# Moving the third row of max scores ahead of the value products in the second attention's loop

## The reference

```python
scores = jnp.einsum('bhqd,bhkd->bhqk', q, k) / math.sqrt(HD)
causal = jnp.tril(jnp.ones((Sx, Sx), dtype=bool))
scores = jnp.where(causal, scores, -jnp.inf)
aw = jax.nn.softmax(scores, axis=-1)
aw = aw.reshape(Bx, NQ, 2, Sx, Sx)
aw = aw[:, :, 0] - lam * aw[:, :, 1]
attn = jnp.einsum('bhqk,bhkd->bhqd', aw, v) * (1.0 - LAMBDA_INIT)
```

## Time and profile before

| | us |
|---|---|
| median of 3 runs | 597.56 (595.37 to 598.63) |
| the profiled execution | 598.44 |
| its span, first to last instruction | 596.7 |

### The profile page before, as it was taken

The page is one execution under the profiler, slowest core; times in us unless marked ns, Lnnn a source line. Parts: engine busy times, 40 slices in busy tenths (PEclk is TensorE's granted clock), DMA queues, the critical chain, the costliest instruction groups (busy, mean ns, idle before and its releaser), DMA issues.

```text
span 596.7 us, 12939 instructions
## 1 busy us (share of the span) xinstructions
PE 515.9 (86%) x3948; PEld 364.4 (61%) x3948; DVE 429.4 (72%) x1668; ACT 328.9 (55%) x544; POOL 311.7 (52%) x472
## 2 busy tenths in 40 slices
PE   4978559967589999999999999998797899999960
PEld 2657459955256444544444544445486799999960
DVE  4785746636859899999999999994859445455436
ACT  4744326622573577777777777775620444454523
POOL 3541055417634586665685667566500577677630
PEclk9998759988699899999999999999969899999995
DMA  8400112322672546557635543431930111111215
GB/s 326 203 2 19 53 37 72 70 75 56 125 133 56 105 99 132 128 108 173 161 80 123 136 120 88 86 80 38 331 102 19 37 49 50 49 48 50 45 33 206
DMA packets 90496, 58.20 MB, mean 98 GB/s; under 512 B 72673, under 2 KB 76770, under 8 KB 88614
## 3 DMA queue, kind: packets, MB, share of 16 engines
q1 hardware_dynamic: 81550, 41.18, 27.4%
q0 software_dynamic: 3744, 7.68, 5.1%
q10 hardware_dynamic: 5136, 8.52, 4.1%
HBM read 37.72 MB, written 19.63 MB: 96 GB/s over the span
## 4 chain that ended last, share of the span: by engine, by line
PE 73%; DVE 15%; DMA 4%; ACT 3%; issue 3%; POOL 2%; ACTq 0%; SPq 0%; POOLq 0%; DVEq 0%
PE banks L1140 15%; PE banks L1984 13%; PE banks L1972 11%; PE banks L1958 11%; PE banks L1153 9%; DVE banks L1675 3%; PE banks L1924 1%; PE banks L1127 1%; PE banks L760 1%; PE banks L363 1%; DVE r_in_place L246 1%; DMA f_hg<-scratch_h_rows,r_source 1%; PE banks L810 1%; PE banks L2065 1%; DMA a_at<-scratch_back_rows,home 1%
## 5 line engine op out<-in xcount | busy, mean ns | idle before, releaser
L1675 DVE CUSTOM_DVE_ANT_1 banks<-banks,a_mask 128x480 f32<-128x480 f32 (+14 forms) x480 | 189.8, 456 | 15.0 <-PE banks L1958 13.2
L1830 ACT ACTIVATE a_prob_<-banks 128x1024 f32<-128x1024 f32 x160 | 154.4, 1021 | 52.6 <-PE banks L1972 52.6
L1506 POOL TENSOR_SCALAR_AFFINE_SELECT a_prob_<-a_prob_ 128x512 f32<-128x512 f32 x128 | 82.1, 645 | 72.6 <-ACT a_prob_ L1830 72.6
L1958 PE MATMUL banks<-a_k_u_,a_q_u_ 72*128 72x512 bf16 (+15 forms) x512 | 103.1, 291 | 4.2 <-DVE a_neg_max_ L1675 4.2
L1958 PEld LDWEIGHTS banks<-a_k_u_,a_q_u_ 72*128 72x128 bf16 x512 | 64.8, 148 | 67.1 <-DVE a_neg_max_ L1675 34.7
L1140 PE MATMUL banks<-f_hgt,f_w_now 128*112 128x128 f32 (+1 forms) x808 | 100.4, 276 | 0.0
L1972 PE MATMUL banks<-a_q_u_,a_k_x_ 75*128 75x512 bf16 x320 | 97.3, 386 | 0.4 <-ACT a_prob_ L1830 0.4
L1140 PEld LDWEIGHTS banks<-f_hgt,f_w_now 128*112 128x112 f32 (+1 forms) x808 | 94.9, 183 | 0.0
L951 POOL DMA_INDIRECT f_hg<-scratch_h_rows,r_source x62 | 59.7, 963 | 61.7 <-DVE r_source L296 32.7
L1984 PE MATMUL banks<-a_prob_,a_v_g_ 128*32 128x512 f32 (+3 forms) x1024 | 83.7, 445 | 2.5 <-POOL a_prob_ L1506 2.5
L1675 DVE DVE_READ_ACCUMULATOR2_ANT a_neg_max_<- 128x1 f32 x512 | 71.1, 140 | 0.0
(11 more groups left out here) (244 smaller groups left out, 690.5 us busy)
## 6 DMA issues: line engine op xcount, KB each, us to landing
a_q_u_<-scratch_q_parts SPq DMA_DIRECT2D x15, 576.0 KB
scratch_o_rows<-a_o_sb_ ACTq DMA_DIRECT2D x28, 256.0 KB, 2.3
w<-in_w SPq DMA_DIRECT2D x2, 2048.0 KB, 10.7
w<-in_w SPq DMA_DIRECT2D x2, 1792.0 KB, 11.5
scratch_q_parts<-a_part_ SPq DMA_DIRECT2D x24, 128.0 KB
a_k_u_<-scratch_k_parts SPq DMA_DIRECT2D x48, 48.0 KB
f_back<-scratch_back_rows SPq DMA_DIRECT2D x4, 512.0 KB, 4.9
w<-in_w SPq DMA_DIRECT2D x2, 896.0 KB, 18.9
```

The costliest lines, as they stand in the source:

```text
L1506: nc.gpsimd.affine_select(out=block_p, in_=block_p, pattern=[[0, JH], [1, P]], compare_op=ALU.is_ge, fill=0.0, base=0, channel_multiplier= ...
L1675: last = nc.vector.tensor_tensor_reduce(out=found, in0=found, in1=mask[:, :, TG - 4 * (t + 1):], scale=-1.0, scalar=-MASKED, op0=ALU.add, ...
L1830: nc.scalar.activation(prob[g % 2][:, 2 * e:2 * e + 2].rearrange("p s j t c -> p (s j) t c"), PS[:, b0:b0 + 2, :].rearrange("p s (j c t) - ...
L1958: last = nc.tensor.matmul(PS[:, a % 3, off:off + width], queries[:, g % 2, :, t], k_u[r][:, :, g % 2 * TG:g % 2 * TG + 4 * (t + 1)], start ...
```

## The change

In the loop, the call that issues row 2 (of the group three ahead) is moved from behind the block of value products to in front of it: TensorE issues row 1, row 2, then `values(g - 1, 1)` to `values(g - 1, 3)`, then scores 2. No instruction is added or removed, and no other engine's order changes. The wait inside `max_scores` moves with the row.

```diff
                 scores(g, 0)
                 rows(0)
                 scores(g, 1)
-                rows(1)
+                rows(1, 2)
                 if g >= 1:
                     for kb in range(1, NQ):
                         values(g - 1, kb)
-                rows(2)
                 if g == GROUPS - 2:
                     second_projection(0)
                     second_projection(1)
```

## The result

The changed kernel takes 613.81 us (median of 4 runs, 612.2 to 613.86), the kernel before 596.46 us beside it: a ratio of 1.0245, with a 95% interval from 1.020 to 1.029. That is 17.35 us more between the medians; the prediction was 11.7 us more. The direction and the mechanism came as forecast, and the loss is larger. On the median of 597.56 that the prediction used, the ratio gives 612.2 us, near the upper end of its range. Medians count every execution of a kernel; ratios and mean clocks leave out the few that ran far longer than the others of the same kernel, three of them above 1000 us.

What follows compares the result with a forecast made beforehand. TensorE's list of work, with its waits, was taken to bound the loop. 23 ordinary iterations at 0.48 us, plus 0.65 and 0.07, gave 11.7 us more: 609.3 us on the median of 597.56, range 603.5 to 613.

Steps and rivals of the forecast that it cites:

- The wait for row 8: On TensorE after row 1: row 2 must wait 0.42 us until VectorE's last read of row 8 frees its bank.
- The new neighbours: TensorE's extras in the new order: row 2 takes 0.34 us, of which 0.09 is the turn to float32; scores 2 takes 0.52.
- That the loss returns each time: Loop from row 8 to row 8: a closed loop of 7.55 us, so 0.48 us is lost in every ordinary iteration.
- The iterations with the factors: Three of iterations 1 to 28: row 3 already waits 0.39 us for VectorE there, so they cost nothing; period 8.10 us.
- VectorE's gap: VectorE's idle 0.35 us ahead of row 2 becomes about 1.0 us ahead of row 3.
- VectorE as the pace-setter: Rival for the loop: closing VectorE's 0.35 us gap makes it faster, by up to 3.3 us, to 594.3 us; chance 0.03.
- The falling clock: Rival: pauses of 0.42 us in each 7.55 us bring TensorE's clock down, 15 us on top, about 624; chance 0.08.
- Iterations 1 and 2: Start of the loop: iteration 1 loses 0.65 us with the clock down, iteration 2 loses 0.07 beside TensorE's wait for POOL.
- The upper end of the range: Total time up to 613 us, for a single further spell of low clock or of longer releases.
- a clock of 1.00 throughout: Sign that the forecast is right: the clock stays at 1.00 throughout.

Runs made afterwards that it cites:

- the repeat: The changed kernel run once more, unaltered, against the kernel before: 615.08 us, ratio 1.0256.
- kernel with the wait alone: Against the kernel before, only the wait for the end of row 8 moved ahead of the value products, row 2 staying behind them: 610.14 us, ratio 1.0168.

## Why the prediction was right, and where its sum was off

**The wait for row 8: right.** Predicted 0.42 us, measured 0.43, released by VectorE 0.06 us after the end of row 8. In another order of rows, the same place without that wait costs the period nothing (though the total some 5 us, at a lower mean clock), and that wait without the change costs 0.32 of the 0.43 us.

**The new neighbours: one of three was wrong.** Row 2 at 0.34 us was right. Scores 2 was put at 0.52, with 0.06 for standing behind the value products; it took 0.46, so that extra doesn't show for scores. That makes the iteration 7.50 us and not 7.55, and the 23 iterations 9.9 us instead of 11.0.

**That the loss returns each time: right.** The period is 7.50 us in all ordinary iterations from 3 on. The iterations with the factors were put at no loss and went from 8.10 to 8.17 us.

**VectorE's gap: right in place.** About 1.0 us ahead of row 3 was predicted, 0.82 measured.

**The rivals.** VectorE as the pace-setter fell: its gap ahead of row 2 was closed without a wait, its idle time came back larger ahead of row 3, and the period rose to 7.31 us with TensorE alone on the chain. The chain before the change and this run agree on that, though no run took much work off VectorE. The falling clock didn't come in the steady loop: waits of 0.43 us in every 7.50 us left it at 1.00 from 219 to 436 us.

**Iterations 1 and 2: the step that was mis-sized.** They were put at 0.65 and 0.07 us, the waits alone. That holds for the repeat in which the clock came back early, and the sum for the loop then came out at 11.2 us against 11.7. That this is so near is partly luck: the ordinary iterations lost 9.9 us and not 11.0, while the iterations with the factors lost some 0.2 us that was not counted, and 0.25 us comes from where the stretch ends. In the first profile, the iterations up to the block of iteration 3 lost 6.5 us, where 0.65 + 0.07 + 0.48 = 1.2 had been counted. The clock was named as a rival, but as a fall in the middle of the loop, priced at 15 us; there it stayed at 1.00 through every wait. It was in iteration 1, where the clock was down before the change too (0.50 from 200 to 202 us), that it stayed down longer. The upper end of the range, set for a single further spell of low clock, had room for that; the sum had no term for it. Of the signs named as right, a clock of 1.00 throughout failed for this stretch.

**What stays open.** The 2.45% are shown as 1.53% from iteration 2 on, near the waits' sum, and 0.81% from iteration 1, more than its wait. Why TensorE's clock comes back later with row 2 in front isn't settled. In 11 of the 13 profiles the clock falls in scores 1 or row 1 of iteration 1 (at 199.3 us, in row 1, before; at 201.3, in scores 1, in the changed kernel), ahead of the moved row, and it falls there in kernels without the move too; so there the move can only prolong it. It did, to some 17 us at 0.50 against 3.4 in the short stretches, in four of five profiles with row 2 in front in iteration 1 and the old order of rows, and in none of the five profiles of that order with row 2 elsewhere in iteration 1. The kernel with the wait alone (0.50 us ahead of that block) had a short stretch, the one with row 1 ahead of scores 1 a long one. When the loop starts may matter too. The four long stretches belong to profiles in which values(0, 0) started between 196.16 and 197.23 us; the repeat and the kernel with the wait alone, both with that wait and a short stretch, started it at 198.89 and 198.57. Without a wait there, the kernels with row 2 in front from iteration 2 on and with row 2 in the middle of the block started it at 196.02 and 196.38 and had short stretches. So at like starts the wait made the difference, and with a late start it didn't; these are few profiles. Why runs reach the loop at different times was not followed up: the first profiles of before and after differ by 2.4 us before the loop and by 3.3 us, the other way, behind it, in parts of the program that the change doesn't touch.

## What to carry to other kernels

Before a piece of work is moved forward in an engine's list, look up the wait that moves with it: what was covered where it stood may be bare at the new place, and all that is queued behind it waits as well, here 0.43 us in each iteration. A gap on a busy engine is worth closing only if that engine is on the chain; here VectorE was busy for 47.45 of 50 us, and closing its gap ahead of row 2 only moved it ahead of row 3, and made the loop longer in two ways, by a wait (7.50 us) and by a block that was cut in two (7.31). To judge whether a wait will be bare, compare the two ways from the last common point, here 3.10 us on VectorE against 2.68 on TensorE. A wait in a stretch where the clock is already low can cost more than its length: iteration 1, whose wait was put at 0.65 us, cost 4.8.

## What the runs showed of the hardware

TensorE's granted clock stayed at 0.50 for 12 us (204 to 216) in which the profile of the changed kernel has TensorE busy for 12.00 of 12.00 us. Cutting a block of float32 value products in two cost 0.13 us (1.57 against 1.44, each piece up to the start of the work behind it, so with a second turn from float32 back to bf16 in it). The turn from bf16 to float32 took a further 0.09 us (before, from row 1 to the block 0.29 us where the columns take 0.20), and didn't show when it fell into a wait (7.39 us against the expected 7.49).
